# A graph and attention layer on one core: edge segments summed inside the last pass, second bias by addition, kind differences by ScalarE

## What is computed

```python
xn = layernorm(x)
# graph part: mean of the edges of each source node, then a small network
sums   = segment_sum(edge_attr, src, 6250)
counts = segment_sum(ones, src, 6250)
agg    = sums / maximum(counts, 1)
g = relu(concat([xn, agg, u]) @ W1 + b1) @ W2 + b2
# mixer part: 4 layers on all nodes as one sequence
for i in range(4):
    h = layernorm(m) * ln1_g + ln1_b
    m = m + linear_attention(h)           # softmax over features (q) and over the sequence (k)
    h = layernorm(m) * ln2_g + ln2_b
    m = m + (gelu(h @ W1[i] + b1[i]) @ W2[i] + b2[i])
x = x + g + m
# then each node goes through the one of 32 small experts that its router picks
```

## Time and profile before

| | |
|---|---|
| runs, median of 3 | 3442.88 us (3442.71 to 3443.29) |
| the profiled execution, time | 3441.36 us |
| its span in the trace | 3439.6 us |
| mean granted TensorE clock | 0.853 |
| busy: PE, PEld | 3046.5 us (89%), 2733.4 us (79%) |
| busy: DVE, ACT, POOL | 2089.6 us (61%), 1542.7 us (45%), 1735.9 us (50%) |
| the indirect transfers of the edges (L701) | 850, 1049.7 us busy on POOL |

### The profile page before, as it was taken

How to read it: one execution, slowest core, us unless ns; L and a number is a source line. 1 busy time by engine, 2 the same in 40 slices (tenths; PEclk the granted TensorE clock), 3 DMA queues, 4 the chain that set the end, 5 groups by cost and what they waited for, 6 DMA issues and landing times. The chain is left out here.

```text
span 3439.6 us, 58754 instructions
## 1 busy us (share of the span) xinstructions
PE 3046.5 (89%) x18957; PEld 2733.4 (79%) x18958; DVE 2089.6 (61%) x4591; ACT 1542.7 (45%) x2948; POOL 1735.9 (50%) x1560
## 2 busy tenths in 40 slices
PE   4888999999899999899999989998788889971598
PEld 2676899999789999799999979998677778861366
DVE  8886566666566666556666644444899945532243
ACT  0433566565365655355556534443222234440243
POOL 0011487777688887688888200002899900004444
PEclk7998999999899999899999999999555579955555
DMA  3001222222323322322322010001533321001232
GB/s 107 27 27 39 72 64 62 65 58 54 91 61 65 68 67 58 91 61 60 69 66 61 26 31 17 18 19 50 142 117 117 97 56 31 16 1 50 81 81 64
DMA packets 248371, 206.68 MB, mean 60 GB/s; under 512 B 156877, under 2 KB 187314, under 8 KB 248141
## 3 DMA queue, kind: packets, MB, share of 16 engines
q1 hardware_dynamic: 180174, 142.74, 15.2%
q0 software_dynamic: 57600, 41.75, 6.2%
q10 hardware_dynamic: 10368, 19.17, 2.0%
HBM read 136.29 MB, written 70.16 MB: 60 GB/s over the span
## 5 line engine op out<-in xcount | busy, mean ns | idle before, releaser
L701 POOL DMA_INDIRECT edges_sorted<-staging,pos_i x850 | 1049.7, 1235 | 249.4 <-issue 230.8
L1273 DVE TENSOR_TENSOR hidh_lo<-hid,hidh_hi 128x500 fp32r<-128x500 f32 x400 | 272.4, 681 | 510.1 <-ACT hidh_hi L812 505.4
L346 PE MATMUL bank<-h_hi,w_hi 128*128 128x250 f32 x1600 | 480.7, 300 | 16.6 <-DVE h_lo L1269 16.5
L346 PE MATMUL bank<-w_hi,hidh_hi 128*125 128x256 f32 x1600 | 478.8, 299 | 0.0
L806 ACT ACTIVATE hid<-bank,b1p 128x250 f32<-128x250 f32 x800 | 332.3, 467 | 305.4 <-PE bank L346 284.3
L346 PE MATMUL bank<-h_hi,w_lo 128*128 128x250 f32 x1600 | 452.6, 283 | 0.0
L346 PE MATMUL bank<-w_lo,hidh_hi 128*125 128x256 f32 x1600 | 451.2, 282 | 0.0
L346 PE MATMUL bank<-w_hi,hidh_lo 128*125 128x256 f32 x1600 | 449.8, 281 | 0.0
L346 PE MATMUL bank<-h_lo,w_hi 128*128 128x250 f32 x1600 | 449.5, 281 | 0.0
L679 POOL TENSOR_TENSOR r<-ve,minus_half 125x2 f32<-125x2 f32 x175 | 134.4, 768 | 598.5 <-DVE ve L1245 595.5
L346 PE MATMUL bank<-wqk,h 128*125 128x256 f32 x1600 | 381.0, 393 | 0.6 <-ACT mbc L857 0.6
(11 more groups left out here) (295 smaller groups left out, 5987.1 us busy)
## 6 DMA issues: line engine op xcount, KB each, us to landing
staging<-in_edge_attr SPq DMA_DIRECT2D x50, 531.2 KB
queries<-qn SPq DMA_DIRECT2D x100, 250.0 KB
qin<-queries SPq DMA_DIRECT2D x100, 250.0 KB
edges_sorted<-staging,pos_i POOLq DMA_INDIRECT x850, 3.5
rows_in<-edges_sorted SPq DMA_DIRECT2D x41, 260.0 KB, 2.8
staging<-edges_sorted SPq DMA_DIRECT2D x40, 260.0 KB, 2.8
yin<-tokens_sorted SPq DMA_DIRECT2D x81, 127.0 KB
rows_in<-edges_sorted ACTq DMA_DIRECT2D x36, 260.0 KB, 2.7
```

What stands on the lines that cost most here:

```text
L346: return nc.tensor.matmul(o, left, right, start=start, stop=stop, skip_group_check=True)
L701: nc.gpsimd.indirect_dma_start(out=edges_sorted, out_offset=bass.IndirectOffsetOnAxis(ap=pos_i[:, i:i + 1], axis=0), in_=stage[:, slot, j, ...
L1273: nc.vector.tensor_tensor(hidh[c % 2][1][:, :, :], hid[c % 2][:, :, :], f32(hidh[c % 2][0][:, :, :]), ALU.subtract).then_inc(f_lo, 1)
```

## The change

Three things are changed.

1. **Segments inside the last pass.** `step(3, t)` has six turns (`SEG_STEP`) on each engine. In turn n ScalarE casts segment n, GpSimd takes its low part, VectorE adds segment n - 4 to `agg` and makes `oh` of n, TensorE multiplies n - 2. Turns 150 to 156 follow behind the pass. All segment loads are SP's, six buffers, four of them in `staging`. The sums use two PSUM banks (`PK`, `PG`). Clearing `agg` and the first loads wait for the last layer's context (`c_ready`) and the last stored queries (`q_out`). The SBUF places of many tiles are moved for it.
2. **Second bias by addition.** The two matmuls, `b2row` and `ones_r` go. VectorE adds the broadcast bias `b2_b` to `res` behind `attention_low`, in all four layers (`add_bias`).
3. **`kb` on ScalarE**, as an Identity activation with the bias `minus_kind`.

Also moved: the graph weights, then the inputs, then `fw1` are loaded when the last segment has been added.

```diff
-RIN = 8
-AHEAD = 5
+RIN = 6
+SEG_STEP = 6
-        SEG_BANK = [PS, PM, PQ, PQT]
+        SEG_BANK = [PK, PG]
...
@@ SP @@
+                sp.wait_ge(b2_added, l * GROUPS)
+                sp.dma_start(b2_b[:, :], mb2[l:l + 1, :].to_broadcast((P, D))).then_inc(w_b2, 16)
...
+            def load_segments(t):
+                if t == -1:
+                    for slot in range(2):
+                        sp.wait_ge(SCATTERED[slot], 16 * CH * (CHUNKS // 2))
+                    sp.wait_ge(spare_written, 16)
+                    sp.wait_ge(r_table, 1)
+                    sp.wait_ge(c_ready, LAYERS)
+                    sp.wait_ge(q_out, 16 * ALL)
+                    for n in range(RIN):
+                        load_segment(sp, n)
+                for n in seg_turns(t):
+                    if n + RIN < ESEGS:
+                        load_segment(sp, n + RIN)
...
             sp.wait_ge(f_res, ALL)
+            sp.wait_ge(s_add, ESEGS)
+
             sp.dma_start(raw_g1[:, 0:2, :], gW1[0:D, :].rearrange("(k p) n -> p k n", p=128)).then_inc(gw_raw, 16)
...
@@ ScalarE @@
+            def seg_hi(n):
...
+                act.wait_ge(S_IN[n % RIN], 16 * (n // RIN) + 16)
+                if n >= 4:
+                    act.wait_ge(s_pe, n - 3)
+                nc.scalar.copy(ehl[n % 4][:, :, 0:EA], rows_in[n % RIN][:, :, 0:EA]).then_inc(s_hi, 1)
...
+                ident_act(kb[:, n % 4, :], rows_in[n % RIN][:, :, EA], bias=minus_kind[:, n:n + 1]).then_inc(s_kb, 1)
...
@@ VectorE @@
+            def add_bias(l, g):
+                dve.wait_ge(w_b2, 16 * (l + 1))
+                dve.wait_ge(a_xh, nth(l, g) + 1)
+                nc.vector.tensor_tensor(pair(res, g), pair(res, g), b2_b[:, :].unsqueeze(1).to_broadcast((P, PAIR, D)),
+                                        ALU.add).then_inc(b2_added, 1)
...
+            def seg_turn(n):
+                if n >= 4:
+                    if n % 3 == 1:
+                        seg_kinds.update(zip(range(n - 4, n - 1), seg_tiles(n - 4, 3)))
+                    seg_add(n - 4, seg_kinds[n - 4])
+                if n < ESEGS:
+                    seg_prep(n)
...
@@ TensorE @@
-                        pe.wait_ge(b2_rows, 2 * l + 2)
...
-                    for j in range(PAIR):
-                        mm(PY[0:P, j * D:(j + 1) * D], ones_r[:, :], b2row[:, :], j == 0, False)
...
+            def segment(n):
+                if n == 0:
+                    pe.wait_ge(s_ones, 5)
+                pe.wait_ge(s_oh, n + 1)
+                pe.wait_ge(s_lo, n + 1)
+                if n >= 2:
+                    pe.wait_ge(s_add, n - 1)
+                for j in range(SEGR):
+                    a = mm(SEG_BANK[n % 2][0:P, 0:2 * EA + 2], oh[n % 4][:, j, :], ehl[n % 4][:, j, :], j == 0, j == SEGR - 1)
+                a.then_inc(s_pe, 1)
...
```

More of the change, by code:

```diff
@@ L61 @@
 SPARE_P = SPARE // 2
-BROW = 33
 XPIECE = 25
@@ L173, in build @@
         xh1 = sb("xh1", [P, PAIR, D], F32, layers)
-        xh2 = [sb(f"xh2_{i}", [P, PAIR, D], F32, layers) for i in range(XR)]
-        kr = [sb(f"kr{i}", [P, PAIR, D], F32, layers) for i in range(KR)]
         h1 = both("h1", [128, KC, GT], layers)
-        h2 = sb("h2", [128, KC, GT], F32, layers)
         qT = sb("qT", [128, KC, GT], F32, layers)
@@ L219, in build @@
         fw1 = sb("fw1", [128, KC, EXP * EH])
-        seg_place = ExitStack()
-        oh = [sb(f"oh{i}", [128, SEGR, P], F32R, seg_place) for i in range(4)]
-        ehl = [sb(f"ehl{i}", [128, SEGR, 2 * EA + 2], F32R, seg_place) for i in range(4)]
-        seg_place.close()
         fw2 = sb("fw2", [EH + 1, EXP * D])
         gnn = ExitStack()
-        agg = sb("agg", [P, TILES, 2 * EA + 2], F32, gnn)
         g1 = both("g1", [128, 3, GH], gnn)
@@ L607, in _ @@
             sp.dma_start(rw_in, rw).then_inc(rw_raw, 16)
-            sp.wait_ge(s_pe, ESEGS)
+            for k in range(KC):
+                sp.dma_start(fw1[:, k, :].rearrange("p (e h) -> p e h", h=EH),
+                             fW1[:, k * 128:(k + 1) * 128, :].rearrange("e p h -> p e h")).then_inc(f_w, 16)
             sp.dma_start(fw2[0:EH, :].rearrange("p (e h) -> p e h", h=D), fW2.rearrange("e p h -> p e h")).then_inc(f_w, 16)
@@ L906, in step @@
                     down_high(l)
+                segs = seg_turns(t) if l == LAYERS - 1 else ()
                 if forward:
-                    gelu(l, t, 0)
-                    gelu(l, t, 1)
-                    gelu(l, t, 2)
+                    for c in range(3):
+                        for n in segs[c:c + 1]:
+                            seg_hi(n)
+                        gelu(l, t, c)
+                for n in segs[3:4]:
+                    seg_hi(n)
                 if later and t >= 1:
@@ L914, in step @@
                     gelu(l, t, 3)
+                for n in segs[4:]:
+                    seg_hi(n)
                 if later and t in MAX_AT:
@@ L948, in _ @@
             passes(step, drain)
[L951 to L970 removed]
+            for n in range(SEG_STEP * GROUPS, ESEGS):
+                seg_hi(n)
             act.wait_ge(gw_raw, 80)
@@ L2025, in _ @@
             passes(step, drain)
-            pe.wait_ge(s_ones, 5)
-            def segment(n, slot):
-                pe.wait_ge(s_oh, n + 1)
-                pe.wait_ge(s_lo, n + 1)
-                if not (isinstance(n, int) and n < 4):
-                    pe.wait_ge(s_add, n - 3)
-                for j in range(SEGR):
-                    a = mm(SEG_BANK[slot][0:P, 0:2 * EA + 2], oh[slot][:, j, :], ehl[slot][:, j, :], j == 0, j == SEGR - 1)
-                a.then_inc(s_pe, 1)
-            for n in range(4):
-                segment(n, n)
-            with pe.Fori(1, ESEGS // 4) as q:
-                for slot in range(4):
-                    segment(4 * q + slot, slot)
-            segment(ESEGS - 1, 0)
+            for n in range(SEG_STEP * GROUPS, ESEGS + 2):
+                seg_turn(n)
             pe.wait_ge(s_add, ESEGS)
```

292 lines of the change are left out of this document (144 added, 148 removed).

## The result

The changed kernel takes 3468.5 us (median of 4 runs, 3467.4 to 3470.1), the kernel before, run beside it, 3442.8 us (4 runs, 3441.9 to 3443.3): ratio 1.0075, 95% interval 1.0058 to 1.0093. It is slower by 0.75%; 3262 us was predicted. The profiled execution has a span of 3467.3 us, before 3439.6.

The account below looks back on a forecast made before the run. A segment stage after the last pass, overlapping nothing, was taken to cost 362.6 us. From 3439.6: - 362.6 - 46 (bias) + 198 (pass) + 3 + 10 (its ends) + 18 (loads) = 3260, adjusted to 3262 us; range 3195 to 3335.

Parts of the forecast that it names:

- The longest loop that I find starts at the addition of turn 1: Last pass: a chain through TensorE, ScalarE and VectorE sets the step, 23.3 us, taken as 23.5.
- the pass: The last pass with the segments inside takes 583 us instead of 385, +198 us.
- TensorE's need: Last pass: TensorE needs 20.4 us a step, 15.38 less 0.62 for the bias plus six segments of 0.94.
- VectorE's own work: Last pass: VectorE needs 21.8 us a step, including 1.3 for loading tile numbers.
- the segment: Last pass: a segment's eight matmuls take TensorE 0.94 us at full clock, 0.117 us apart.
- The bias: Layers 0 to 2: dropping two matmuls saves TensorE 0.62 us in each of 75 steps, 46 us (30 to 46).
- I cost it at nothing: Layers 0 to 2: the added VectorE bias addition, 0.68 us, is hidden, as VectorE has 7 us free in 20.
- The loads: After the last segment: graph weights, inputs and `fw1`, no longer covered by the segment stage, cost +18 us (8 to 30).
- (2): Last pass: GpSimd stops VectorE longer, step 24.4 or 26, or bias addition not hidden earlier; 3285 to 3325 us; chance 0.25.
- (3): Last pass: the clock falls; 3600 us if all at 1.2 GHz, break-even at a 30.7 us step; chance 0.09.
- (1): Last pass: VectorE and GpSimd seldom lock, `oh` near 1.19 us, step 21.0 to 21.5, 3205 us; chance 0.15.
- the signs that I gave for a wrong forecast: Pass clock under 0.9; VectorE waiting for ScalarE or segment loads; TensorE idle over 40 us before the graph stage.

Follow-up runs that it names:

- e3: The changed kernel with ScalarE casting and making `kb` one segment ahead: 3264.9 us, ratio 0.9482 to the kernel before.
- e5: The changed kernel with VectorE adding segment n - 3 instead of n - 4 to `agg` in turn n: 3297.0 us, ratio 0.9579 to the kernel before.
- e8: The changed kernel with `kb` made on GpSimd again, ScalarE making only the cast: 3261.2 us, ratio 0.9479 to the kernel before.
- e10: The changed kernel, ScalarE one segment ahead, `agg` addition one segment earlier, GpSimd filling `ehl`'s low part with zeros, reading nothing: 3178.8 us.
- e2: The kernel before with the second bias by addition and 10 instead of 12 edge transfers a step in layers 1 and 2: 3371.5 us.
- e9: The changed kernel, ScalarE one segment ahead, addition one earlier, 11 transfers a step in layers 1 and 2, inputs loaded before `fw1` and `fw2`: 3201.5 us.
- e6: The changed kernel with GpSimd filling `ehl`'s low part with zeros, so that it reads nothing: 3319.7 us, ratio 0.9645 to the kernel before.
- e7: The changed kernel with 24 filling matmuls more a step of the last pass, before TensorE's sixth segment: 3422.6 us, ratio 0.9946 to the kernel before.

## Why the prediction was wrong

**The step that failed** is the loop between the engines, "The longest loop that I find starts at the addition of turn 1", with 23.3 us. It sent `kb` behind the gelu at turn 4 alone and ran VectorE's `agg`, `oh`, `h_lo`, bias, `agg`, `oh`, residual, `agg` through without a stop. In the trace two of three turns have such a wait on ScalarE (97 of some 145 `oh`, 179 us), and TensorE, which I also ran through, stops for `agg` three times a step (72 times, 187 us; 1.93, 3.90 and 2.16 in one step). From the addition of turn 5 to that of turn 1 this was 6.5 us in my sum (2.61 + 2 x 1.96), and it takes 10.65, since `h_lo` stands behind TensorE's segment of the same turn, and the `oh` of turn 0 behind `qT`. The step was off by 7.1 us, 24 x 7.1 = 171 of the 175 us by which the pass missed. Read off the trace as a mean of 21 steps, the stretches of the predicted loop are:

| from, to | predicted | measured |
|---|---|---|
| addition of turn 1 (0.28) to the fourth gelu, over TensorE | 10.4 | 13.0 |
| fourth gelu to `oh` of turn 4, on ScalarE | 2.35 | 2.9 |
| `oh` of turn 4 to the addition of turn 5, on VectorE | 3.4 | 4.3 |
| addition of turn 5 to that of turn 1 | 7.2 (6.5 + a tile load) | 10.5 |
| loop | 23.3 | 30.7 |

The first and the last hold most of the miss (5.9 us), and both have waits for something that another engine makes in the same turn, with the half clock that follows one of them; the third is the long `hidh_lo`. e3, e5 and e8 show that it is the loop: each opens it at one place and takes the step to 22.3 to 23.7, about what I had forecast. That they land there is in part luck, since at this step other terms are at work than in my sum (TensorE's need is 19.0, and the stops cost 2.4).

**The other terms of the step** were nearer. VectorE's own work: 496.36/730 x 30.62 = 20.8 us. Predicted were 21.8, of which 1.3 was standing still for tile loads; the changed kernel's pass shows no such wait, so 20.5 is the number to compare, and 20.8 has the stops of `hidh_lo` in it. TensorE's need: 19.0 (e10), predicted 20.4. In the timeline of e10 the eight matmuls of a segment take 2300.76 - 2299.85 = 0.91 us at full clock, predicted 0.94:

```profile
2299.85 1.07 PE L352 MATMUL bank<-ehl,oh 128*125 128x130 f32 x8
2300.76 0.33 PE L352 MATMUL bank<-h_hi,w_hi 128*128 128x250 f32 x1
```

So the segment was right, and the rest of the step, which I put at 14.76, is 19.02 - 6 x 0.91 = 13.6: in the pass of before TensorE was idle for 16.6 of 382 us, 0.7 a step, and such gaps are filled in e10; 0.1 is the step I read, 15.38 for a mean of 15.26. The remaining 0.4 is open. `kb` takes 0.30 to 0.31, predicted 0.2; that is not what makes the delay.

**The bias** was mis-sized: -46 predicted, -12.7 found up to the first `up`. Layer 0 gave 9.3 of some 15: its first to last residual took 482.9 us before, 473.6 after. TensorE's busy time in it did fall by 14.2 (482.96 of 483 to 468.76 of 474), and it idles now for 5. "I cost it at nothing" looked at VectorE's room alone and took layer 0's row for layers 1 and 2. GpSimd was already full there, 394.8 us busy and 78 between transfers in 487, in the kernel before. e2 gains 38 us by relieving it, of which some 25 are the bias's share by the sum above.

**The loads** were right in size (+16.6, predicted +18), not in mechanism. I put it on the bytes. SyncE's queue shows that the third input is issued only 23 us after the first loads, most of it the issue of `fw1` and `fw2`:

```profile
2765.16 0.39 SPq L599 DMA_DIRECT2D raw_g<-in_L_gnn_W  x1
...
2770.86 9.87 SPq L613 DMA_DIRECT2D fw<-in_L_ffn_W  x2
2780.79 4.43 SPq L616 DMA_DIRECT2D fw<-in_L_ffn_W  x1
...
2788.25 1.96 SPq L608 DMA_DIRECT2D staging<-in_x  x2
```

My sum put that input 37 us behind the last addition, and it is used 36.8 behind it (2801.88 - 2765.08): the size agrees by luck. And e9, in which the wait is gone, ends only 4.8 us earlier. The larger part is the wait for the graph weights, which nothing covers any more: from the last addition into `agg` to the first input added to `res` are 3.0 us before (2753.99 to 2756.97) and 14.2 after (2765.08 to 2779.26).

**The rivals.** (2), longer stops, had the right mechanism: `hidh_lo` does meet GpSimd (0.68 to 1.65 us), and e6 prices the stops at 5.8 a step in the closed ring. But its largest step was 26. (3) named 30.7 us as the step from which the change loses, and the step is 30.6; that is chance, as the cause is another, and e7 gives the clock some 2 us of it. That 30.6 already loses comes from the missing 33 us of the bias. (1) fell: 1.86 us is the mean `oh`, not 1.19. Two of the signs that I gave for a wrong forecast were there: the clock under 0.9, and ScalarE as what VectorE waits for.

What stays open: how much of the 9.2 us between ring closed and open is waiting itself and how much the clock that comes with it, and a way to make `ehl`'s low part that stops nobody; it was not tried.

## What to carry to other kernels

When a stage is interleaved into another, write down for every turn the operation in front of it on each in-order engine, and follow releases around all engines, turn by turn. If what an engine makes in a turn is used by the next engine in the same turn and so on around, all can wait though none is full; one segment of lead, put in on ScalarE, on VectorE or by way of GpSimd, was worth 5 to 6% here (on TensorE it was not tried). Busy shares and sums by engine can't show it. An edit that frees the bounding engine is worth at most what the second-fullest engine of that very stretch leaves, so read it stage by stage.
